# Gated cross-attention with a routed MoE: where the expert row buffers are zeroed, and by what kind of DMA

## The reference

```python
q = fq_sym((layernorm(x) @ Wq + bq) * scale)          # 127 steps per head and token
k, v = fq_sym(ctx @ Wk + bk), fq_sym(ctx @ Wv + bv)   # v: 127 steps per column
attn = fq_unsigned(softmax(q @ k.T))                  # 255 steps per row
x = x + tanh(g_xattn) * (attn @ v @ Wp + bp)
scores = softmax(layernorm(x) @ Wg.T)                 # 16 experts in 4 groups
# top 2 groups, top 4 experts in them, weighted sum of silu(h W1) * (h W3) W2
# plus a shared expert of twice the hidden width
x = x + tanh(g_ffn) * (routed + shared)
```

## Time and profile before

| what | value |
|---|---|
| median of 3 runs | 1085.31 us (1083.11 to 1085.69) |
| the profiled execution, its own time | 1084.69 us |
| its span (first to last instruction) | 1083.1 us |
| busy: PE, DVE, ACT, POOL | 988.3, 643.7, 500.8, 460.8 us |
| mean granted clock of PE | 0.975 of full speed |
| DMA: moved, mean | 172.45 MB, 159 GB/s |

### The profile page before, as it was taken

One profiled execution on the slowest core, in us unless ns is written; L12 is line 12 of the kernel. 1 busy time (PEld: TensorE's weight loads), 2 busy tenths in 40 slices (PEclk: granted clock), 3 DMA queues, 4 the chain that ended last, 5 costly groups with the idle time before them and its releaser, 6 DMA issues.

```text
span 1083.1 us, 16600 instructions
## 1 busy us (share of the span) xinstructions
PE 988.3 (91%) x5718; PEld 499.6 (46%) x5719; DVE 643.7 (59%) x1140; ACT 500.8 (46%) x1072; POOL 460.8 (43%) x352
## 2 busy tenths in 40 slices
PE   5999999879998888998999689999999999999993
PEld 2334444324333333343344356555556556566551
DVE  4895676599998888998899646731111111111146
ACT  2022222369999898998999732111212212212110
POOL 1043333237888787787777700072111111111165
PEclk9999999989999999999999878999999999999996
DMA  9931332588999999999787544053546645643155
GB/s 316 227 97 78 109 105 82 122 169 153 192 189 195 201 194 185 205 203 165 130 136 113 91 168 165 1 204 117 185 155 227 212 173 221 218 170 135 48 159 154
DMA packets 264496, 172.45 MB, mean 159 GB/s; under 512 B 239344, under 2 KB 239344, under 8 KB 262128
## 3 DMA queue, kind: packets, MB, share of 16 engines
q1 hardware_dynamic: 250016, 124.67, 49.3%
q0 software_dynamic: 14416, 46.94, 13.3%
HBM read 68.67 MB, written 44.63 MB: 105 GB/s over the span
## 4 chain that ended last, share of the span: by engine, by line
PE 50%; POOL 21%; DVE 13%; issue 8%; ACT 5%; DMA 2%; SPq 0%; POOLq 0%; DVEq 0%; ACTq 0%
PE ps L685 17%; POOL arena_a L1344 16%; PE ps L705 10%; PE ps L553 6%; PE ps L530 5%; PE ps L570 4%; ACT arena_a L859 3%; DVE span_max L1044 3%; POOL expert_in L1356 2%; PE ps L655 2%; PE ps L612 2%; POOL expert_in L1348 2%; PE ps L715 1%; DVE v_q L1265 1%; PE ps L696 1%
## 5 line engine op out<-in xcount | busy, mean ns | idle before, releaser
L1044 DVE TENSOR_REDUCE span_max<-ps 128x1 f32<-128x481 f32 (+2 forms) x400 | 351.4, 904 | 34.7 <-PE ps L570 28.0
L859 ACT ACTIVATE arena_a<-ps,exp_bias,q_step 128x962 uint8<-128x962 f32 (+1 forms) x288 | 329.9, 1156 | 35.0 <-PE ps L570 15.0
L1344 POOL CAST arena_a<-arena_a 128x3072 bf16<-128x3072 uint8 x100 | 274.3, 2748 | 115.6 <-DMA arena_a<-arena_a 110.2
L570 PE MATMUL ps<-arena_a,q_t 128*128 128x481 bf16 (+1 forms) x864 | 223.1, 372 | 18.6 <-DVE span_max L1044 8.9
L685 PE MATMUL ps<-arena_a,xt 128*128 x544 | 172.3, 459 | 1.7 <-issue 1.7
L1203 DVE TENSOR_TENSOR proj_d<-ps,proj_f 128x352 f32<-128x352 f32 x48 | 25.1, 524 | 205.5 <-ACT proj_f L894 205.4
L705 PE MATMUL ps<-arena_a,proj_r 128*128 (+3 forms) x288 | 134.0, 602 | 0.7 <-ACT proj_r L900 0.7
L900 ACT COPY proj_r<-ps 128x128 f32<-128x128 f32 x144 | 28.4, 270 | 227.1 <-PE ps L696 227.1
L570 PEld LDWEIGHTS ps<-arena_a,q_t 128*128 128x128 bf16 x864 | 62.2, 97 | 147.3 <-ACT arena_a L859 67.2
L685 PEld LDWEIGHTS ps<-arena_a,xt 128*128 128x128 f32 x544 | 100.5, 190 | 61.1 <-issue 17.8
L612 PE MATMUL ps<-v_q,arena_a 128*128 128x32 bf16 (+1 forms) x2400 | 80.2, 180 | 22.7 <-POOL arena_a L1344 20.7
(11 more groups left out here) (168 smaller groups left out, 958.5 us busy)
## 6 DMA issues: line engine op xcount, KB each, us to landing
arena_a<-in_w_up SPq DMA_DIRECT2D x18, 1408.0 KB, 6.4
arena_a<-in_w_down SPq DMA_DIRECT2D x18, 768.0 KB, 8.4
key_parts<-parts SPq DMA_DIRECT2D x23, 512.0 KB, 2.6
expert_in<-proj_r POOLq DMA_DIRECT2D x42, 256.0 KB, 3.6
xt<-expert_in POOLq DMA_DIRECT2D x36, 256.0 KB, 3.0
expert_out<-xt POOLq DMA_DIRECT2D x34, 256.0 KB, 2.3
arena_a<-in_ctx_t SPq DMA_DIRECT2D x3, 1536.0 KB, 13.7
expert_out<-proj_r POOLq DMA_DIRECT2D x17, 256.0 KB, 3.0
```

The costliest lines, as they stand in the source:

```text
L570: last = mm(ps[:, bank + b, 0:w], q_t[:, head, t * P:(t + 1) * P], k_t[head % NK][:, a:a + w], start=True, stop=True)
L859: nc.scalar.activation(halves[:, :, a:a + w], ps[:, bank:bank + 2, 0:w], ACT.Exp, bias=exp_bias[:, n % 2:n % 2 + 1], scale=step_of, accum_ ...
L1044: v.tensor_reduce(span_max[:, n % 2, j:j + 1], ps[:, bank:bank + len(blocks), 0:w], AX.XY, ALU.max).then_inc(s_max, 1)
L1344: p.tensor_copy(p_t[n % NPT].rearrange("p c q -> p (c q)").rearrange("p (j i) -> p j i", j=2), pt_u8[n % NT8].rearrange("p (i j) -> p j i" ...
```

## The change

A new tensor in memory, `zero_rows`, holds one tile of zeros (256 KB). POOL clears `proj_r[:, 0]` as its second instruction and stores it there. In the loop over key tiles SP issues, behind each key store, one or two copies from `zero_rows` into the expert buffers, each over ZSTEP = 2 tiles, the source repeated by a broadcast; 30 copies in all, 29 of two tiles and a last one of one tile. POOL's memset behind the keys and its 59 stores in attention are gone. At the first key tile SP and POOL wait for the store of `zero_rows`.

```diff
-        ZEROED = [(expert_in, a) for a in range(MAXT + 1)]
-        ZEROED += [(expert_out, a) for a in range(MINT, MAXT + 1)]
+        zero_rows = nc.dram_tensor("zero_rows", [P, D], f32, kind="Internal").ap()
+        ZSTEP = 2
+        ZEROED = [(expert_in, a, min(ZSTEP, MAXT + 1 - a)) for a in range(0, MAXT + 1, ZSTEP)]
+        ZEROED += [(expert_out, a, min(ZSTEP, MAXT + 1 - a)) for a in range(MINT, MAXT + 1, ZSTEP)]
...
                 sp.dma_start(key_parts[kt * P:(kt + 1) * P, :],
                              parts[:, (T + kt) % 2].rearrange("p h g d -> p (h g d)")).then_inc(s_kp[(T + kt) % 2], 16)
+                if kt == 0:
+                    sp.wait_ge(s_zrow, 16)
+                for rows, a, n in ZEROED[len(ZEROED) * kt // KT:len(ZEROED) * (kt + 1) // KT]:
+                    sp.dma_start(rows[a * P:(a + n) * P, :].rearrange("(j p) d -> j p d", j=n),
+                                 zero_rows.unsqueeze(0).to_broadcast([n, P, D])).then_inc(s_xz, 16)
...
             p.memset(x_sb[:, T - 1, :], 0.0).then_inc(s_pad, 1)
+            p.memset(proj_r[:, 0, :], 0.0).then_inc(s_zero, 1)
...
+            pool.dma_start(zero_rows, proj_r[:, 0, :]).then_inc(s_zrow, 16)
...
+                if kt == 0:
+                    pool.wait_ge(s_zrow, 16)
                 pool.wait_ge(s_kd, kt + 1)
...
-            pool.wait_ge(s_mid, KT)
-            pool.wait_ge(s_parts, KT)
-            p.memset(proj_r[:, 0, :], 0.0).then_inc(s_zero, 1)
-            pool.wait_ge(s_zero, 4)
...
-                if 8 <= n < 8 + len(ZEROED):
-                    rows, a = ZEROED[n - 8]
-                    pool.dma_start(rows[a * P:(a + 1) * P, :], proj_r[:, 0, :]).then_inc(s_xz, 16)
```

More of the change, by code:

```diff
@@ L306, in gated_xattn_moe_kernel @@
         s_zero = sem("zeros_ready")
+        s_zrow = sem("zero_rows_stored")
         s_xz = sem("expert_in_zeroed")
@@ L1312, in _ @@
             p.iota(iota_i[:, :], [[1, MAXT]], base=0, channel_multiplier=0).then_inc(s_zero, 1)
-            pool.wait_ge(s_zero, 2)
+            pool.wait_ge(s_zero, 3)
             p.tensor_copy(tile_no[:, :], iota_i[:, :]).then_inc(s_zero, 1)
-            pool.wait_ge(s_zero, 3)
+            pool.wait_ge(s_zero, 4)
             p.tensor_scalar(thresholds[:, :], tile_no[:, 1:T], float(P), None, ALU.mult).then_inc(s_pool, 1)
+            pool.dma_start(zero_rows, proj_r[:, 0, :]).then_inc(s_zrow, 16)
             for kt in range(KT):
```

## The result

The change makes the kernel slower: 1245.46 us (median of 6 runs, 1244.79 to 1247.17) against 1084.56 us (1081.53 to 1085.82), a ratio of 1.149 with a 95% interval of 1.147 to 1.152. The forecast was 1549, range 1264 to 1616: the right sign, and a size that the range does not hold.

What follows compares the result with a forecast made beforehand. PE was read as busy eight to nine tenths nearly everywhere, with DMA engines full in attention. The sum: 1084.7 + 0.5 (early store) + 481.6 (late attention start) - 18 (attention's gain) = 1549 us, range 1264 to 1616.

Steps and rivals of the forecast that it cites:

- Two engines: K and V projections: each pair copy, slowest index 2, runs on 2 of 16 engines, each moving 256 KB.
- The signs named for the profile: Profile after: projections some 600 us, DMA share 0.15 to 0.2, key stores landing after tens of us, attention tiles 3.7 us.
- The stage lasts as long as their work: Projections: the two copying engines never run dry and set the stage's length; attention starts at 695.6 instead of 214.0, +481.6 us.
- I take 20 us, near turns and near that row: Projections: price of one pair copy, near reading and writing in turn (22.3 us) and the full mixed stretch (21.2 us).
- second rival: Projections: copies on two engines with reading and writing overlapped, 12.1 us each, 1320 in all, or 1264 at 10.2; chance 0.24.
- The lower bound: Projections: cheapest pair copy, 10.2 us at the storing rate of 25.7 GB/s an engine, giving the range's low end of 1264.
- Attention's gain: Attention, tiles 11 to 75: removing 59 issues and 15.5 MB of stores saves 18.3 us, taken as 18.
- reasoning by two buffers: Attention: two transpose buffers, each holding a 4.7 us transpose then a 2.75 us cast, give 3.73 a tile over ACT's 3.67.
- The fourth rival: Attention: key loads alone cause the delays, so no gain; adds up to 18 us, 1088 with copies hidden; spread without gain 0.02.
- First rival: Projections: copies spread over all engines, at most 2.8 us each, hidden by the stores' slack; 1070; chance 0.12 with a gain.
- the 2.7 us at the first keys: Start of attention, spread case: the last copies stand ahead of the first keys, making them up to 2.7 us late at PE.
- Everything after attention at nothing: After attention: no cost, since ACT's and POOL's waits for all zeros come long after the copies.

Runs made afterwards that it cites:

- c16: Changed kernel with each zero copy written with 16 shares at its slowest index, same bytes and queue; 1069.61 us against 1082.79, ratio 0.987.
- z4: Changed kernel with ZSTEP = 4, so 14 copies of four tiles, one of two and one of one; 1120.13 us (one run).
- s2far: Against sb, two-tile zero stores put on 2 engines, in 2 KB rows read from on-chip partitions 0 and 64; 1287.05 us (one run).
- c2r: Changed kernel with pair copies still on 2 engines, but in rows of 2 KB instead of runs of 64 KB; 1261.44 us (one run).
- b4: Kernel before the change, its zeroing in attention in 16 stores of up to 4 tiles instead of 59 of one; 1105.23 us, ratio 1.022.
- z1: Changed kernel with ZSTEP = 1: 59 copies of one tile each, written as 16 x 4096 words; 1070.61 us against 1085.06, ratio 0.988.
- sb: Changed kernel with zeros stored by SP from a cleared on-chip bias row instead of copied from memory; 1069.40 us against 1082.79, ratio 0.987.

## Why the prediction was right, and where wrong

- **Two engines: right.** c16 and z4 show it from both sides, and the share of 0.20 between the transposes is that of two engines. The Trainium skill's rule on the slowest dimension (DMA: Bandwidth & Descriptors, "Rules for kernel authors") agrees: 2 gives 9.66 us for 512 KB, 4 gives the same for 1 MB, 16 gives 1.55 us for 512 KB.
- **The signs named for the profile: most, not all.** ACT waits for `key_parts`, key stores land after 17.9 us (median; tens were named), tiles of attention take 3.73 us with transposes landing after 4.0. But the projections stretch to some 330 us and not 600, and over the whole stage the DMA share is 0.63 and not 0.15 to 0.2, because it reads near one where a transpose of values waits (last section). The trace gives no landing for the pair copies.
- **"The stage lasts as long as their work": right.** With the measured copy the same sum reads 62.3 + 29 x 9.66 (280) + 32 + 13 + 8.3 = 395.7; the first score came at 390.6. Of these 5 us the stores' share, 1.25 us instead of 1.4, explains 3.
- **"I take 20 us, near turns and near that row": the step that failed.** The term 29 x 20 = 580 measured 280, and this is nearly the whole miss: 1549 - 300 = 1249 against 1245.5. A copy costs what a store does (s2far, c2r), not a load and a store in turn. The row at share 1.00 with 12.4 GB/s an engine was no price for a copy. In that window 21,116 of 21,763 packets are under 512 bytes, and its queues differ (packets, MB, share of 16 engines over 40 us; q1 holds the transposes, q0 the stores of zeros):

```profile
q1 hardware_dynamic: 20955, 5.23, 79.5%
q0 software_dynamic: 803, 2.63, 19.5%
```

  By these, transposes move 10.3 GB/s an engine and the stores of zeros 21.1, so the 12.4 is mostly the price of transposes. At 21.1 GB/s the 262,144 bytes are 12.4 us, near the second rival's copy.
- **The lower bound failed too.** 10.2 us came from 25.7 GB/s, a rate of 16 engines and of a share printed to two digits (0.19; the rounding leaves room up to 26.5). Two engines alone reach 27.1. The bound should have left room for an engine that has more to itself than one of sixteen. 0.54 us per copy, times 29, is 16 of the 18.5 us by which the time lies under the range.
- **The second rival had the better cost** (reading and writing overlapped) and still was slow: 1320 at 12.1 us, 1264 at 10.2. Its sign was key tiles at 16 to 18 us on average; from key tile 2 to 22 they took 14.1.
- **Attention's gain: right**, 18.3 forecast, 18.1 measured, 17.8 in c16; and as forecast the transposes land sooner. The gain was read from the rows of the late tiles. The reasoning by two buffers alone, 3.73 over 3.67 us a tile, would give only 4 us over 64 tiles, so it does not explain the 18. The fourth rival (key loads are enough to cause the delays) falls: with key loads and no zeroing tiles 11 to 75 take 3.73 us each, with delays left only at group changes. b4 adds what the reasoning by two buffers did not have: the size of one store matters beside the sum.
- **First rival, copies spread: 1070 forecast for that case, 1069.6 measured.** That it is so close is luck in part: the 2.7 us at the first keys did not appear (0.3), and 2 us after attention did.
- **"Everything after attention at nothing": off by 2 us**, and the cause stays open (last section).

## What to carry to other kernels

Before moving a DMA, read the shape that the built program carries: a broadcast or tile index put outermost can leave it on as few engines as that index counts, and whatever else needs those engines waits behind it, in the same queue or in another. Put an index divisible by 16 outermost. Price a DMA by bytes per engine for the number of engines it runs on, from long runs alone; and zeroing that must happen somewhere belongs in a stage whose DMA share is low, in pieces small enough not to stand ahead of a latency-bound transfer.

## What the runs showed of the hardware that was not expected

- A copy from memory to memory reached 27.1 GB/s an engine on 2 engines, and 21.1 each on 16, in smaller pieces (338 GB/s in each direction); 2 KB rows instead of 64 KB runs cost 6%.
- Two engines reading on-chip partitions 0 and 1 took some 21.5 us for 256 KB each; from partitions 0 and 64, 9.92 us. Why is not shown; a shared way out of neighbouring partitions would fit.
- A DMA share near one need not mean moving data. Behind the copies a transpose of values was issued over 35 us (before: 4.1), and in that stretch the share reads 0.99 at 101 GB/s. Around the next one, from 248 to 284 us, it reads 1.30 at 73 GB/s, so it is not a share of busy time there:

```profile
162.00:216.00 54.00, 31.83 (x59) 13.22 (x60) 20.33 (x34) 7.14 (x12) 10.52 (x8) 0.78 0.99 101
```

```profile
168.07 1.25 SPq L425 DMA_DIRECT2D expert_in<-zero_rows  x2
169.37 35.01 SPq L412 DMA_TRANSPOSE v_q<-arena_b  x1
```

- After attention the kernels differ by up to 3 us, and why is open. From tile 99's first exponential to the span's end it takes 471.7 us in the kernel before, 473.8 in the changed kernel and in c16, but 472.2 in z1, whose attention is as quick, and 472.0 in b4, whose attention is the slowest; sb has 474.6. In the 8 us that begin 64 us behind that exponential PE's granted clock was 0.92 before, 0.93 in z1 and 0.91 in b4, and in the other kernels 0.74 (sb) to 0.89. That the clock's later return costs those 2 us would fit, but one execution of each kernel was profiled and it was not tested.
